# Graph layer of a two-layer GNN on one core: the degree factors spread over rows, and the adjacency collected by nodes, with DMA transfers instead of TensorE products

## The reference, cut to what matters

```python
GROUPS = [list(range(25)), [0, 1, 2, 3, 4, 5, 6, 7, 8], [0, 9, 10, 11, 12, 13, 14],
          [6, 7, 8, 12, 13, 14], [3, 4, 5, 9, 10, 11]]
def _graph_conv(x, adj, W, b):
    A = adj + jnp.eye(n, dtype=adj.dtype)
    deg = jnp.sum(A, axis=-1)
    dinv = jnp.where(deg == 0, 0.0, deg_safe ** (-0.5))
    norm_adj = dinv[:, :, None] * A * dinv[:, None, :]
    support = jnp.einsum('bnd,de->bne', x, W)
    out = jnp.einsum('bnm,bme->bne', norm_adj, support) + b
    return jax.nn.relu(out)
for g, idx_list in enumerate(GROUPS):
    h = _graph_conv(x[:, idx, :], adj[:, idx][:, :, idx], W1[g], b1[g])
    out_g = _graph_conv(h, adj_g, W2[g], b2[g])
    fused = fused.at[:, idx, :].add(norm_w[g] * out_g)
x = _layernorm(x + fused)
```

## Time and profile before

| | before |
|---|---|
| runs | 366.38 us median of 3 (366.36 to 367.81) |
| the profiled execution: time, span | 365.84 us, 364.0 us |
| mean granted TensorE clock | 0.997 of full speed |
| busy: PE, DVE, ACT, POOL | 346.3 us (95%), 325.9 (90%), 233.9 (64%), 66.9 (18%) |
| DMA | 30.25 MB, mean 83 GB/s |

### The profile page before, as it was taken

The page is one execution under the profiler, slowest core; times in us unless marked ns, Lnnn a source line. Parts: engine busy times, 40 slices in busy tenths (PEclk is TensorE's granted clock), DMA queues, the critical chain, the costliest instruction groups (busy, mean ns, idle before and its releaser), DMA issues. The chain is left out here.

```text
span 364.0 us, 6144 instructions
## 1 busy us (share of the span) xinstructions
PE 346.3 (95%) x1806; PEld 293.9 (81%) x1806; DVE 325.9 (90%) x595; ACT 233.9 (64%) x392; POOL 66.9 (18%) x107
## 2 busy tenths in 40 slices
PE   4989999999999999999999999999999999999894
PEld 2677879968998789978997889978997899776673
DVE  3999999998999999999999899998999899996536
ACT  4382685749674886659584876669584966376761
POOL 6900004020010302030201202030202009041013
PEclk9999999999999999999999999999999999999998
DMA  8706220505141402313140513221150413111001
GB/s 233 256 1 191 78 69 11 176 1 144 41 132 42 140 20 76 125 51 93 40 144 29 144 40 87 86 89 55 40 173 0 144 40 117 42 61 35 29 2 51
DMA packets 28250, 30.25 MB, mean 83 GB/s; under 512 B 3985, under 2 KB 17225, under 8 KB 28233
## 3 DMA queue, kind: packets, MB, share of 16 engines
q1 hardware_dynamic: 27770, 29.93, 27.1%
q10 hardware_dynamic: 462, 0.12, 0.1%
HBM read 24.85 MB, written 4.40 MB: 80 GB/s over the span
## 5 line engine op out<-in xcount | busy, mean ns | idle before, releaser
L1225 POOL TENSOR_TENSOR rs<-base,cst 128x5 f32<-128x5 f32 x16 | 23.8, 1489 | 277.6 <-DVE base L1358 277.6
L991 ACT ACTIVATE am<-ring 128x512 f32<-128x512 f32 x56 | 31.8, 597 | 25.5 <-PE ring L653 25.5
L1322 DVE TENSOR_TENSOR am<-am,adj 128x512 f32<-128x512 f32 x64 | 40.5, 685 | 2.3 <-ACT am L991 2.3
L653 PE MATMUL p_outer<-t_h,w_h 128*128 128x344 f32 x131 | 41.0, 328 | 1.5 <-DVE wc L1377 0.8
L653 PE MATMUL p_outer<-t_h,w_l 128*128 128x344 f32 x131 | 40.3, 322 | 0.6 <-DVE w_l L1446 0.6
L1502 DVE TENSOR_TENSOR am_l<-am,am_h 128x2048 fp32r<-128x2048 f32 x15 | 34.3, 2288 | 2.3 <-ACT am_h L1092 2.3
L1004 ACT ACTIVATE n_h<-ring 128x512 fp32r<-128x512 f32 x16 | 9.6, 599 | 32.5 <-PE ring L653 32.4
L653 PE MATMUL ring<-right,left 128*128 128x512 f32 x62 | 26.3, 427 | 3.0 <-ACT am L991 2.5
L653 PE MATMUL p_middle<-t_h,w_h 128*128 128x344 f32 x90 | 28.6, 329 | 0.4 <-DVE rz L1452 0.4
L1092 ACT ACTIVATE am_h<-am 128x2048 fp32r<-128x2048 f32 x15 | 28.5, 1900 | 0.0
L653 PE MATMUL p_middle<-t_h,w_l 128*128 128x344 f32 x90 | 28.0, 322 | 0.0
(11 more groups left out here) (333 smaller groups left out, 980.0 us busy)
## 6 DMA issues: line engine op xcount, KB each, us to landing
adj<-adjT SPq DMA_DIRECT2D x64, 256.0 KB, 3.1
xpad<-xT SPq DMA_DIRECT2D x17, 256.0 KB, 3.1
out<-yoo SPq DMA_DIRECT2D x16, 256.0 KB, 2.3
wc<-w_c SPq DMA_DIRECT2D x2, 384.0 KB, 4.5
right<-left SPq DMA_DIRECT2D x16, 48.0 KB
wraw<-g_w SPq DMA_DIRECT2D x1, 640.0 KB
wc<-g_w SPq DMA_DIRECT2D x1, 640.0 KB, 4.4
wraw<-w_ih SPq DMA_DIRECT2D x1, 384.0 KB, 6.1
```

The lines of the kernel that those rows point to most:

```text
L653: return nc.tensor.matmul(out_, w, x, start=start, stop=stop, skip_group_check=True)
L991: A(am[:, c, :], R_D[c][:], ACT.Exp).then_inc(s_e[c], 1)
L1225: TT(rs[:], base[:], cst[:, C_MH:C_MH + CH + 1], ALU.pow).then_inc(s_rs, 1)
L1322: TT(am[:, c, :], am[:, c, :], adj[:, c, :], ALU.mult).then_inc(s_am[c], 1)
```

## The change

The factors are no longer spread by products. `dinv` goes to a DRAM buffer `factors` and comes back as `across`, all 106 x 8 numbers in each of 106 rows, in the place in `he` that `diag` had. SP issues both in pass 14. DVE multiplies `ac` with it in one operation over all eight pairs, with `across` read transposed (column by pair becomes pair by column); it stands in pass 14 between mask 2 and mask 3. Outside the blocks `ac` is zero, so that a factor may stand on any row.

The collection by nodes is done by copying: POOL zeroes `msel`, and 16 DMA transfers, issued by SP in pass 15, copy each run of rows of each group from `ac` to its nodes' rows of `msel`. RUNS lists them: one run for groups 0 and 1, two for the other three; for both batches of the pair that makes 2 x 8. The two ACT copies go. The first aggregation waits for these transfers (s_msel at 256) and for s_w0 and s_w2, for which `spread` had waited.

```diff
-        diag = part(he[:], 0, CC, CC)
+        across = he[:].rearrange("p a b -> p (a b)")[0:CC, 0:PAIRS * CC].rearrange("p (c j) -> p c j", j=PAIRS)
+        factors = nc.dram_tensor("factors", (CC, PAIRS), fp32).ap()
-            def spread(self, pe, mm):
-                pe.wait_ge(s_diag, 2)
-                for h in range(2):
-                    mm(BC_BANKS[h][0:CC, 0:HP * CC], cst[0:CC, C_SAME:C_SAME + CC], diag[:, pairs(h), :]).then_inc(s_spread, 1)
-            def combine(self, pe, mm):
-                for h in range(2):
-                    pe.wait_ge(s_columns, h + 1)
-                    mm(MSEL_BANKS[h][0:64, 0:HP * CC], cst[0:CC, C_SELT:C_SELT + 64], ac[0:CC, pairs(h), :]).then_inc(s_combined, 1)
...
             def columns(self, dve):
-                for h in range(2):
-                    dve.wait_ge(s_spread, h + 1)
-                    nc.vector.tensor_tensor(ac[0:CC, pairs(h), :], ac[0:CC, pairs(h), :], banked(BC_BANKS[h], CC, CC), ALU.mult).then_inc(s_columns, 1)
+                dve.wait_ge(s_scaled, 1); dve.wait_ge(s_spread, 16)
+                nc.vector.tensor_tensor(ac[0:CC, :, :], ac[0:CC, :, :], across[:].rearrange("p c j -> p j c"), ALU.mult).then_inc(s_columns, 1)
...
+            def by_node(g, q):
+                at = GOFF[g] + q * len(GROUPS[g])
+                for i, m, rows_ in RUNS[g]:
+                    sp.dma_start(msel[SLOT * q + m:SLOT * q + m + rows_, :, group(g)], ac[at + i:at + i + rows_, :, group(g)]).then_inc(s_msel, 16)
...
                     sp.dma_start(gw1, g_w1.rearrange("g p h -> p g h")).then_inc(s_gw1d, 16)
+                    sp.wait_ge(s_columns, 1); sp.wait_ge(s_mzero, 1)
+                    for g, q in itertools.product(range(NG), range(2)):
+                        by_node(g, q)
...
+                if static(b, B - 2):
+                    sp.wait_ge(s_dinv, 2)
+                    sp.dma_start(factors[:, :], dinv[:]).then_inc(s_row, 16)
+                    sp.wait_ge(s_row, 16); sp.wait_ge(s_t3h, PAIRS); sp.wait_ge(s_t3l, PAIRS)
+                    sp.dma_start(across, factors.unsqueeze(0).to_broadcast([CC, CC, PAIRS])).then_inc(s_spread, 16)
...
-                if static(b, B - 1):
-                    pe.wait_ge(s_w0, PAIRS); pe.wait_ge(s_w2, PAIRS)
-                    g_pe.spread(pe, mm)
...
-                    pe.wait_ge(s_msel, 2)
+                    pe.wait_ge(s_msel, 2 * 16 * sum(len(r) for r in RUNS)); pe.wait_ge(s_w0, PAIRS); pe.wait_ge(s_w2, PAIRS)
...
-                else:
-                    g_act.combined(act)
...
-                    pool.wait_ge(s_t3h, PAIRS); pool.wait_ge(s_t3l, PAIRS)
                     TT(dinv[:], dg[:, 3, :], dg[:, 0, :], ALU.mult).then_inc(s_dinv, 1)
                     pool.wait_ge(s_dinv, 2)
-                    TT(diag[:], cst[0:CC, C_ID:C_ID + CC].unsqueeze(1).broadcast_to([CC, PAIRS, CC]),
-                       dinv[:].unsqueeze(2).broadcast_to([CC, PAIRS, CC]), ALU.mult).then_inc(s_diag, 1)
-                    TT(ac[0:CC, :, :], ac[0:CC, :, :], dinv[:].unsqueeze(2).broadcast_to([CC, PAIRS, CC]), ALU.mult).then_inc(s_diag, 1)
+                    TT(ac[0:CC, :, :], ac[0:CC, :, :], dinv[:].unsqueeze(2).broadcast_to([CC, PAIRS, CC]), ALU.mult).then_inc(s_scaled, 1)
+                    pool.wait_ge(s_t3h, PAIRS); pool.wait_ge(s_t3l, PAIRS)
+                    nc.gpsimd.memset(msel[:], 0.0).then_inc(s_mzero, 1)
...
                 for c in range(CH):
+                    if static(b, B - 2) and c == CH - 1:
+                        g_dve.columns(dve)
                     mask(n, 1, c)
```

More of the change, by code:

```diff
@@ L226, in gnn_kernel @@
         s_out = [sem(f"s_out{p}") for p in range(2)]
-        s_spread = sem("s_spread"); s_columns = sem("s_columns"); s_combined = sem("s_combined"); s_msel = sem("s_msel")
+        s_row = sem("s_row"); s_spread = sem("s_spread"); s_columns = sem("s_columns"); s_msel = sem("s_msel"); s_mzero = sem("s_mzero")
         s_gathered = sem("s_gathered"); s_agT = sem("s_agT"); s_first = sem("s_first"); s_hid0 = sem("s_hid0"); s_hid1 = sem("s_hid1")
@@ L257, in gnn_kernel @@
         gst = sb("gst", [64, PAIRS, 6]); gmv = sb("gmv", [64, PAIRS, 2]); gbase = sb("gbase", [64, PAIRS]); grs = sb("grs", [64, PAIRS])
-        s_bias = sem("s_bias"); s_zz = sem("s_zz"); s_diag = sem("s_diag"); s_hz = sem("s_hz")
+        s_bias = sem("s_bias"); s_zz = sem("s_zz"); s_scaled = sem("s_scaled"); s_hz = sem("s_hz")
         s_gmv = sem("s_gmv"); s_gbase = sem("s_gbase"); s_grs = sem("s_grs"); s_gst = sem("s_gst")
-        BC_BANKS = MSEL_BANKS = (p_outer, p_middle)
         TR_BANKS = (p_outer, p_middle, p_z)
@@ L369, in gnn_kernel @@
         class GroupsAct:
-            def combined(self, act):
-                for h in range(2):
-                    act.wait_ge(s_combined, h + 1)
-                    nc.scalar.activation(msel[:, pairs(h), :], banked(MSEL_BANKS[h], 64, CC), ACT.Copy).then_inc(s_msel, 1)
             def channels(self, act, i):
@@ L635, in _ @@
             batches(sp, step)
-            sp.wait_ge(s_combined, 2); sp.wait_ge(s_aml, B - 1)
+            sp.wait_ge(s_aml, B - 1)
             sp.dma_start(ac[CC:CC + NG, :, :], consts[0:NG, C_G5T:C_G5T + CC].unsqueeze(1).broadcast_to([NG, PAIRS, CC])).then_inc(s_bias, 16)
@@ L875, in odd @@
                 gate(p_gi, "n", 0, cb_h, cb_l, True, False)
-                if static(b, B - 1):
-                    g_pe.combine(pe, mm)
                 if more:
@@ L1532, in odd @@
                     rows_val(n, 0)
-                if not more:
-                    g_dve.columns(dve)
                 mask_low(n)
```

## The result

| | before | changed |
|---|---|---|
| median of 4 runs | 366.37 us (365.94 to 367.81) | 371.87 us (370.62 to 371.98) |
| ratio, 95% interval | | 1.0135, 1.010 to 1.017 |
| profiled execution: time, span | 365.84, 364.0 us | 371.85, 370.0 us |
| mean granted TensorE clock | 0.997 | 0.983 |

A forecast was written before the change was run, and what follows sets the result against it. PE's chain bounds from 320.81 us, DVE before it. PE alone gives 3.0, the stall 1.3; DVE's wait for the factors cuts the gain to 2.8: 366.38 - 2.8 = 363.6 us, range 362.9 to 368.5.

The forecast's parts named there:

- The collection: Sixteen SP transfers into msel from 323.95, 0.41 us each, landing at 331.9, before the 332.8 needed to cost nothing.
- case 3: Rival: each SBUF-to-SBUF copy costs SP 0.80 us, PE waits before the aggregation until 337.75; 368.5 us, chance 0.18.
- The granted clock is 1.00 already, so nothing comes or goes by it: PE in the last passes: no gain or loss from the TensorE clock, already at 1.00.
- PE's four products: Chain before the first aggregation: four plain-fp32 p_outer and p_middle products go, 2.99 us; neighbour product ends about 331.8.
- POOL and DVE: Pass 14: scaling replaces diag, L1335's stall stays, L1339's 1.40 us goes, memset harmless; both engines 1.3 us earlier.
- The spread factors: Load of across on two DMA engines, 1.5 plus 7.4 to 8.2 us, landing at 322.6; DVE waits 0.6 us.
- Case 4: Rival: factors late, two engines at half or three quarters rate, landing 330 or 325.2; say 366.2 us, chance 0.11.
- The product on DVE: Before mask 3: one strided 848-element operation takes 1.35 us, between 1.03 and 2.07, ending at 323.95.
- nb and yoo: Statistics 2.2 us earlier, nb at 334.9 instead of 337.07; yoo begins with nb, 2.8 us earlier.

The follow-up runs named there:

- e3: Changed kernel with the sixteen copies of same destinations, rows and widths read from the adjacency in DRAM instead of ac in SBUF: 363.64 us, ratio 0.9945.
- e2: Changed kernel with eight of its sixteen copies, those of the last two groups (three rows each) left out: 365.38 us, ratio 0.994.
- e4: Changed kernel with 22 additional unread products of PE in front of the wait for msel: 369.81 us, ratio 1.0078.
- e7: Changed kernel, copies where they are, with factors stored pair by pair and across loaded in 96 and 10 rows: 374.05 us, ratio 1.019.
- e1: Changed kernel with the collection back on PE and ACT (two products, two copies), factors still spread by transfers: 365.93 us, ratio 0.9976.
- e5: Changed kernel with the copies issued early, in pass 14, and two DVE products, msel behind am_l and ac behind n_l: 366.05 us, ratio 0.9991.
- e8: Changed kernel with the eight copies of each pair's second batch issued by POOL instead of SP: 364.50 us, ratio 0.9929.
- e9: Changed kernel with copies early in pass 14, then pair-by-pair factors loaded in 96 and 10 rows, ac's product after nb: 364.04 us, ratio 0.9924.
- e12: Changed kernel with copies issued on two queues (SP and POOL), plus six additional PE products before the W2 products: 364.58 us, ratio 0.9945.

## Why the prediction was wrong, point by point

**The failed step** stands under *The collection*: "These copies resemble the loads in size, number of rows and shape, and `right<-left` in source; I take the loads' figure." It took 0.41 us; 0.78 was measured, 12.54 us for sixteen. The other end of the bound, from the one row with the same source, was 0.80. By e3 the source decides for all but the single rows; by e2 leaving out the three-row copies saves no more than their number. The loads' 0.41 was itself a mean over unlike ones (line L574 in the trace of before: 282/283/674 ns), so that likeness in rows and shape had to be priced shape by shape; in the sum this did no harm, since e3 gave 0.41 again. The text had the right rival (case 3, from 0.66 us on) and gave it 0.18.

**The size of that rival** was short by 3.4 us: 368.5 forecast, 371.87 measured, and so the range missed. Of this 1.2 us is a later aggregation, 338.96 instead of 337.75. The copies started at 325.33 and not at 323.95: the execution was 0.5 us late altogether, the factors landed at 323.3 and not at 322.6 (0.2 with the lateness taken off), and the product took 1.90 us, not 1.35. The rest is the clock, 2.6 us (that the two make 3.8 is because the profiled executions lie 6.0 us apart and the medians 5.5): "The granted clock is 1.00 already, so nothing comes or goes by it" is right for the case without a wait and wrong for the rival, which by its own numbers puts 6 us of idle time (331.8 to 337.75) in front of PE; 5.59 was measured. e4 shows that this fall follows the idle time.

**PE's four products**: 2.99 us went from the chain as said; in the changed kernel PE was ready at 333.37, 2.2 us before 335.58, in an execution 0.5 us late (forecast: 331.8).

**POOL and DVE**: one stall of two gone, the scaling at 4.42 us in the place of `diag`, the memset harmless. All as forecast, and DVE reached the product's place some 1.45 us earlier (1.3 forecast, 1.4 the bound). That the scaling needs 4.42 us here and 2.05 in its old place bears out the reading that POOL stood for DVE during `diag`.

**The spread factors**: 9.45 us from issue to landing against 1.5 + 7.4 to 8.2 forecast; DVE waited 0.97 us against 0.6. The Trainium skill ("DMA: Bandwidth & Descriptors", on the semaphore's 16) gives two engines for 106 rows and 16 for 96; by that rule the split load should land sooner, and the runs agree, with 9.45 us for 106 rows and 5.0 for 96 and 10. Case 4 did not occur.

**The product on DVE**: mis-sized. 1.90 us with the step of eight, 1.04 without it (e7), near the upper bound of 2.07. The interpolation from a step of three was too kind. The Trainium skill ("Advanced Engine Details and Errata", SBUF Cachelines) speaks of a penalty without a figure; here it is 0.86 us for 848 elements.

**nb and yoo**: nb was ready at 336.15, 0.9 us before 337.07, against 2.2 forecast; the difference is the late execution and the product. With msel in time (e3) nb came at 335.3 and the time was 363.64. So the account of what else moved was right in the main, and one price turned its sign. That e3 meets the 363.6 to a tenth is in part luck: the kernel before stood at 366.07 in that set, so by the medians the gain was 2.4 us and not 2.8.

**Still open**: why the clock falls behind 340 us in some executions and not in others of the same program; why late runs of the kernel before (mean clock 0.986 to 0.996 from 368 us on) are late, since no trace of one was taken; why a source in SBUF is dearer to issue; and why one of the early copies held SP for over 3 us.

## What to carry to other kernels

When one operation has two nearest rows that differ by a factor of two, ask which of their properties sets the cost, and do not take the one that resembles it in more ways: here the issue price went by the source for fourteen of sixteen. Look at the spread behind a mean, too. Sixteen small copies are sixteen issues; count them, spread them over two queues, or start them where nobody waits. A wait of several microseconds in front of PE costs its own length and then the time until the clock is back, so a rival with such a wait has to be priced with both.

## What the runs showed of the hardware that was not expected

- SP needed 0.69 to 0.91 us to issue a copy from SBUF to SBUF, even of one row of 8 x 14 numbers. For the same destinations from DRAM it needed 0.41 on the mean: 0.28 for three rows, but 0.64 and 0.70 for a single one. POOL needed 0.63 on the mean for the SBUF copies.
- A store of 106 x 8 numbers to DRAM took 2.35 us as 106 pieces and 9.6 as 848 pieces of four bytes.
- In a wait of 5.59 us PE's granted clock fell to 0.50 and stayed there for some 10 us, with PE busy from 338.96 on. In the traces of e1, e2 and e5 it fell behind an idle place of 1.60 us; in those of e3, e8 and e9, which have the same 1.60 us, it did not; and in that of e12 it fell with PE busy all the time from 350 to 355 us (granted clock 0.68).
- A DVE product with two SBUF inputs held a small POOL operation until it ended (e5: 1.06 us instead of 0.20), the same stall as that of DVE behind POOL, the other way round.
